# Edge scores of a graph attention layer: a one-hot of 112 rows plus 16 rows of block digits, a mask and one maximum, in place of a product and a sum

## What is computed

```python
xp = (layernorm(x) @ W).reshape(N, H, C)          # N = 3125, H = 4, C = 256
a_src = einsum('nhc,hc->nh', xp, att_src)         # one term a node and head
a_dst = einsum('nhc,hc->nh', xp, att_dst)
e = leaky_relu(a_src[src] + a_dst[dst], 0.2)      # a score for each edge and head
m = segment_max(e, dst)
alpha = exp(e - m[dst]) / segment_sum(exp(e - m[dst]), dst)[dst]
out = relu(segment_sum(xp[src] * alpha, dst) + bias)
x = x + out; x = x + moe_ffn(layernorm(x))
```

## Time and profile before

| | us |
|---|---|
| median of 3 runs | 2160.78 (2157.02 to 2161.48) |
| span of the profiled execution, the only time of it that is listed | 2296.1 |
| first stage, to the barrier | 0 to 332 |
| score stage | 332.1 to 482.6 |
| maxima, exponents, rest of the Gram matrix | 483 to about 590 |
| gather, norm, experts | to 2296.1 |

### The profile page before, as it was taken

The page is one execution under the profiler, slowest core; times in us unless marked ns, Lnnn a source line. Parts: engine busy times, 40 slices in busy tenths (PEclk is TensorE's granted clock), DMA queues, the critical chain, the costliest instruction groups (busy, mean ns, idle before and its releaser), DMA issues. The chain is left out here.

```text
span 2296.1 us, 53233 instructions
## 1 busy us (share of the span) xinstructions
PE 1959.2 (85%) x14846; PEld 1318.7 (57%) x14847; DVE 1470.6 (64%) x4341; ACT 1137.3 (50%) x2499; POOL 768.2 (33%) x943
## 2 busy tenths in 40 slices
PE   6999977667878888888888589983899999999997
PEld 4666545645766667777667455652454445555553
DVE  7988859987666666666666699867543443443333
ACT  4444421113666666676666566654543443443332
POOL 1020000022555555555555232321233333333332
PEclk9999976568999999999999889995899999999999
DMA  7444544403988888888888677746646556644542
GB/s 272 134 143 136 172 131 172 186 0 114 312 281 291 286 299 287 294 296 287 287 298 294 235 249 240 228 142 234 233 169 249 212 167 239 221 160 171 176 162 80
DMA packets 135664, 490.15 MB, mean 213 GB/s; under 512 B 16900, under 2 KB 17108, under 8 KB 133410
## 3 DMA queue, kind: packets, MB, share of 16 engines
q0 software_dynamic: 95568, 334.62, 43.5%
q1 hardware_dynamic: 31954, 125.15, 15.1%
q10 hardware_dynamic: 8064, 29.36, 3.7%
HBM read 419.17 MB, written 81.17 MB: 218 GB/s over the span
## 5 line engine op out<-in xcount | busy, mean ns | idle before, releaser
L1130 PE MATMUL main_ps<-rows,O 128*128 128x256 f16 x4992 | 619.2, 283 | 125.7 <-DVE acc L1066 66.3
L1113 ACT ACTIVATE O<-O,pk 128x128 f16<-128x128 f16 x1664 | 502.9, 387 | 246.1 <-DVE O L1083 203.5
L1130 PEld LDWEIGHTS main_ps<-rows,O 128*128 128x128 f16 x4992 | 480.9, 102 | 217.9 <-issue 72.8
L1052 POOL DMA_INDIRECT rows<-projected,idx x416 | 395.5, 951 | 325.2 <-PE small_ps L1135 202.9
L1087 DVE TENSOR_SCALAR O<-O,pk 128x128 f16<-128x128 f16 x1664 | 314.6, 273 | 15.0 <-issue 0.2
L1837 PE MATMUL x_h<-w_p,gram 128*128 x1344 | 307.1, 386 | 18.4 <-ACT gram L1787 7.6
L1852 PE MATMUL x_o<-w_p,gram 128*128 x1344 | 308.0, 379 | 1.4 <-ACT gram L1806 1.4
L1886 PE MATMUL pj_ps<-gram,xsT 128*125 128x512 f16 x1200 | 271.1, 385 | 8.8 <-ACT xsT L402 5.5
L1837 PEld LDWEIGHTS x_h<-w_p,gram 128*128 128x128 f16 x1344 | 131.6, 99 | 171.6 <-issue 31.5
L1886 PEld LDWEIGHTS pj_ps<-gram,xsT 128*125 128x125 f16 x1200 | 163.2, 139 | 104.7 <-ACT xsT L402 8.6
L1083 DVE TENSOR_SCALAR O<-iota,pk 128x128 f16<-128x128 f16 x416 | 109.4, 263 | 164.9 <-PE small_ps L1135 124.1
(11 more groups left out here) (346 smaller groups left out, 2538.9 us busy)
## 6 DMA issues: line engine op xcount, KB each, us to landing
w_f<-in_L_ffn_W_dram SPq DMA_DIRECT2D x14, 2048.0 KB
b_t<-in_L_ffn_b_dram ACTq DMA_DIRECT2D x56, 512.0 KB
projected_f<-xp_f POOLq DMA_DIRECT2D x25, 500.0 KB, 3.7
projected<-xp POOLq DMA_DIRECT2D x25, 500.0 KB, 4.6
out_dram<-n_x SPq DMA_DIRECT2D x25, 500.0 KB
x_after_gnn_normed<-PK POOLq DMA_DIRECT2D x25, 500.0 KB, 9.1
xt<-in_x_dram SPq DMA_DIRECT2D x24, 512.0 KB, 3.3
n_own<-projected_f SPq DMA_DIRECT2D x24, 512.0 KB, 13.0
```

The lines of the kernel that those rows point to most:

```text
L1052: pool.indirect_dma_start(out=rows[:, 4 * p + k, :, :].rearrange("k n d -> k (n d)"), out_offset=None, in_=xp_d[:, :], in_offset=bass.Indi ...
L1113: ins = act.activation(O[:, k, 1 + HEADS + h, :], O[:, k, 0, :], ACT.Copy, scale=pk[:, p, k, w:w + 1])
L1130: pe.matmul(main_ps[:, h * C:(h + 1) * C], O[:, k, 1 + HEADS * a + h, :], rows[:, 4 * p + k, b, h * C:(h + 1) * C], start=first and h % 2 ...
```

## The change

Source nodes are numbered by blocks of 112 rows in place of 125 (28 blocks in place of 25). The one-hot gets all 128 partitions: rows 0 to 111 tell the row in the block, and 16 more rows tell the block by two digits of base 7 (`digits_d`: 8 rows for the block number divided by 7, 8 for the rest). The matrix that it is multiplied with (`terms`) holds the node terms in its first 112 rows and, in the 16 digit rows, -65504 wherever the digit is not the block's (`digit_mask`). So every candidate but the right one comes out hugely negative, and DVE takes one maximum out of 112 columns a visit.

- DVE: the product `pick`, its sum and the eight `high_one_hots` go; one `tensor_reduce` with max reads PSUM directly. New are `digit_mask` (18 small instructions at i = 16), five more instructions in `edge_numbers`, one copy at the stage's end (`terms`); one of three `turned_numbers` goes.
- PE: 112 columns and 128 rows in place of 100 and 125 for each of the 832 source products, a third PSUM buffer for them (it waits for the maximum three groups ago), chunks 2 to 7 written out, 53 small products at the end of the first stage that move `st16` from blocks of 125 to blocks of 112 rows, four transposes fewer.
- SP: each chunk is loaded by three transfers (112, 16 and 128 partitions) in place of two, and two more tables are stored to DRAM.

```diff
-HI = -(-NODES // P)
+LOW, TENS, DIGITS = 112, 7, 8
+HI = -(-NODES // LOW)
+MASK = -65504.0
...
+        def load_numbers(sp, lo, dl, vs, done):
+            sp.dma_start(lo[0:LOW], lo_d[vs, :].partition_broadcast(LOW)).then_inc(done, 16)
+            sp.dma_start(lo[LOW:P], digits_d[:, vs, :].rearrange("n v k -> n (v k)").unsqueeze(1).broadcast_to([2, DIGITS, CHUNK * P])).then_inc(done, 16)
+            sp.dma_start(dl, dloc_d[vs, :].partition_broadcast(P)).then_inc(done, 16)
...
-                        if i in (15, 17, 19):
+                        if i in (15, 17):
                             turned_numbers((i - 15) // 2)
+                        if i == 16:
+                            digit_mask()
-                        if 17 <= i < 25:
-                            high_one_hots(i - 17)
...
+                    dve.wait_ge(s_spread, 1)
+                    dve.tensor_copy(terms[:, :, :, :], spread_ps)
...
+                    pe.matmul(spread_ps, ident16[:, :], mask[:, :, :, :], start=True, stop=True, skip_group_check=True)
+                    for n, blocks in enumerate((range(LATE), range(LATE, BLOCKS))):
+                        pe.wait_ge(s_st16, 2 * n + 2)
+                        for b in blocks:
+                            for a in range(ROWS * b // LOW, (ROWS * (b + 1) - 1) // LOW + 1):
+                                w = P - (ROWS * b - LOW * a)
+                                ins = pe.matmul(spread_ps[0:LOW, :, a, :], shift16[0:ROWS, w:w + LOW], ...
...
-                        for t, d in ((lo_b, lo_d), (dl_b, dloc_d)):
-                            sp.dma_start(t[p], d[CHUNK * i:CHUNK * (i + 1), :].partition_broadcast(P)).then_inc(s_row[p], 16)
+                        load_numbers(sp, lo_b[p], dl_b[p], slice(CHUNK * i, CHUNK * (i + 1)), s_row[p])
...
-                        dve.wait_ge(s_row[p], 32 * (j + 1))
-                        dve.tensor_scalar(lo_b[p], lo_b[p], iota_col[:, 0:1], None, ALU.is_equal)
+                        dve.wait_ge(s_row[p], 48 * (j + 1))
+                        dve.tensor_scalar(lo_b[p], lo_b[p], src_row[:, 0:1], None, ALU.is_equal)
...
-                            dve.tensor_tensor(pick[:, b, :, :, :], s_ps[b]..., hi_oh[:, four(n), :]..., ALU.mult).then_inc(s_sel, 1)
-                        dve.tensor_reduce(sT[:, four(n), :], pick[:, b, :, :, :], AX.X, ALU.add).then_inc(s_got, 1)
+                            dve.tensor_reduce(sT[:, four, :], s_ps[b][:, :, :].rearrange("k v (a h) -> k v h a", h=HEADS), AX.X, ALU.max).then_inc(s_got, 1)
...
-                            if not early(n, 2):
-                                pe.wait_ge(s_sel, n - 1)
+                            if n >= 3:
+                                pe.wait_ge(s_got, n - 2)
...
-                    steps(pe, 8, body)
+                    for i in range(8):
+                        body(i, i // 2, i % 2)
```

More of the change, by code:

```diff
@@ L226, in program @@
         early_ctx = ExitStack()
-        hiT = sbuf(early_ctx, "hiT", [P, VISITS], F16)
-        hi_oh = PK[:, :, :].rearrange("k v n -> k (v n)").bitcast(U8)[:, 0:VISITS * HI].rearrange("k (v a) -> k v a", a=HI)
+        src_row = sbuf(early_ctx, "src_row", [P, 1])
+        terms = sbuf(early_ctx, "src_terms", [P, 2, HI, HEADS], F16)
         dstV = sbuf(early_ctx, "dstV", [VP, ROW4])
@@ L591, in term_parts, with digit_mask @@
                         dve.tensor_tensor(st16[:, bs, 2 * HEADS:], stN[:, bs, :], st16[:, bs, 0:2 * HEADS], ALU.subtract).then_inc(s_st16, 1)
[L593 to L599, removed]
+                    def digit_mask():
+                        dve.memset(shift16[:, 0:P], 0.0)
+                        dve.memset(shift16[:, 2 * P:], 0.0)
+                        dve.tensor_copy(shift16[:, P:2 * P], ident)
+                        link(dve.tensor_scalar(digit[:, 0:1], iota_col[:, :], LOW - 0.5, -float(LOW), ALU.is_gt, ALU.mult))
+                        link(dve.tensor_scalar(digit[:, 1:2], iota_col[:, :], LOW + DIGITS - 0.5, -float(DIGITS), ALU.is_gt, ALU.mult))
+                        link(dve.tensor_tensor(digit[:, 2:3], digit[:, 0:1], digit[:, 1:2], ALU.add))
+                        link(dve.tensor_tensor(src_row[:, :], iota_col[:, :], digit[:, 2:3], ALU.add))
+                        link(dve.tensor_scalar(digits_of[:, 0, :], iota_row[:, 0:HI], 1.0 / TENS, -0.5 * (TENS - 1) / TENS, ALU.mult, ALU.add))
+                        link(dve.tensor_scalar(digits_of[:, 0, :], digits_of[:, 0, :], WHOLE, None, ALU.add))
+                        link(dve.tensor_scalar(digits_of[:, 0, :], digits_of[:, 0, :], -WHOLE, None, ALU.add))
+                        link(dve.scalar_tensor_tensor(digits_of[:, 1, :], digits_of[:, 0, :], -float(TENS), iota_row[:, 0:HI], ALU.mult, ALU.add))
+                        dve.tensor_scalar(digit[:, 3:4], iota_col[:, :], LOW - 0.5, MASK, ALU.is_gt, ALU.mult)
+                        link(dve.tensor_scalar(digit[:, 1:2], iota_col[:, :], LOW + DIGITS - 0.5, None, ALU.is_gt))
+                        link(dve.tensor_tensor(digits_of[:, 1, :], digits_of[:, 1, :], digits_of[:, 0, :], ALU.subtract))
+                        link(dve.scalar_tensor_tensor(digits_of[:, 2, :], digits_of[:, 1, :], digit[:, 1:2], digits_of[:, 0, :], ALU.mult, ALU.add))
+                        link(dve.tensor_scalar(digits_of[:, 0, :], digits_of[:, 2, :], src_row[:, :], digit[:, 3:4], ALU.not_equal, ALU.mult))
+                        for part in range(2):
+                            dve.tensor_copy(mask[:, part, :, :], digits_of[:, 0, :].unsqueeze(2).broadcast_to([P, HI, HEADS]))
@@ L859, in body @@
                                 skip_runtime_bounds_check_because="the table counts the borders at or below a visit, of which there are BLOCKS - 1")
-                            if not early(n, 2):
-                                pe.wait_ge(s_sel, n - 1)
+                            if n >= 3:
+                                pe.wait_ge(s_got, n - 2)
                             for u in range(4):
                                 for part in range(2):
-                                    h0 = 2 * HEADS * part
-                                    pe.matmul(s_ps[(p + q) % 2][:, u, :].rearrange("k (a h) -> k a h", h=HEADS), lo_b[p][0:ROWS, 4 * q + u, :],
-                                              st16[:, :, h0:h0 + HEADS], start=(part == 0), stop=(part == 1))
+                                    pe.matmul(s_ps[n % 3][:, u, :], lo_b[p][:, 4 * q + u, :],
+                                              terms[:, part, :, :].rearrange("r a h -> r (a h)"), start=(part == 0), stop=(part == 1))
                             if not early(n, 2):
```

65 lines of the change are left out of this document (36 added, 29 removed).

## The result

The changed kernel takes 2197.9 us (median of 4 runs, 2192.9 to 2200.6) against 2158.9 us (2156.9 to 2161.5): ratio 1.0173, 95% interval 1.0156 to 1.0191. The forecast was 2171 us, with 2147 to 2180 as its range. The sign was right; the added time is four times the 10.2 us of the sum. The comparisons here therefore use e1.

What follows compares the result with a forecast made beforehand. DVE seemed to bind the score stage, with the load's landing cycle right behind. Score stage +6.7 us and first stage +3.5 gave +10.2 us on 2160.8, so 2171 us, range 2147 to 2180.

Steps and rivals of the forecast that it cites:

- The sign: Whole kernel: slower than before the change, given a chance of 0.62.
- The view of the cycle: Score stage: a faster DVE uncovers load issue, landing, one-hots, last groups, next load; period = landing + 5.6 us.
- The engine count: Digits' load in each chunk: carried by two DMA engines, not sixteen, showing 34 small packets a chunk; chance 0.69.
- The landing: Chunk loads: two engines carry seven rows more, +3.5 to +3.9 us, so landing 14.6 us (13.8 to 15.7).
- the rival: Digits' load spread over all sixteen engines: landing 11.5 us, period 17.1, kernel 2149 us (2143 to 2153); chance 0.22.
- Chunks 1 to 6: Score stage: period 20.2 us for 18.06 in six chunks, +12.8 us (+8 to +19.4).
- Chunk 0: Score stage's first chunk: load landed long before its one-hots, one group less stands behind, -1.4 us.
- Chunk 7: Score stage's last chunk, no load to wait for: PE's groups 0.94 us apart, 12.8 us for 17.5, -4.7.
- The maximum: DVE's one reduce a group in the score stage, 448 values from PSUM: 0.62 to 0.64 us.
- the rival of a slow read: DVE's maximum, read from PSUM with stride four, takes 1.1 us: +4 us on the forecast; no chance of its own.
- The first stage: Stage before the scores: build_first waits for a later two-engine landing, +3.5 us (+3 to +5); on sixteen engines 0.
- the forecast's case at its dearest: Upper end of the two-engine case for the whole kernel: +18 us, 2179 us; chance of two engines 0.69.

Runs made afterwards that it cites:

- e1: The kernel before the change, unchanged, a single profiled run beside the others: 2161.1 us.
- e10: Changed kernel without the digits' load, low numbers broadcast to all 128 partitions, so its scores are wrong: 2145.9 us.
- e9: Changed kernel, both number tables broadcast to 128 partitions, 16 digit rows loaded over partitions 112 to 127 once the low numbers landed; local one-hots first: 2155.3 us.
- e3: Changed kernel with the digits loaded by two loads of 8 partitions, one for each table, in place of one: 2178.5 us.
- e12: Changed kernel with the same three loads of a chunk, the two-engine digits' load moved last, behind the local numbers: 2171.1 us.
- e4: Changed kernel with each digit stored eight times, as a table of 16 rows, so the digits' load is on sixteen engines: 2164.6 us.
- e2: Kernel before the change, with only the broadcast of the low numbers split into loads of 112 and 16 partitions: 2178.5 us.
- e7: Kernel before the change, with the broadcast of the low numbers split into two loads of 64 partitions: 2185.5 us.
- e5: Changed kernel with low numbers and digits in one table of 16 rows, loaded to 128 partitions by one load, each row repeated 8 times: 2181.0 us.
- e11: As e9, but the digits of chunks 1 to 7 issued from POOL's queue and the low numbers' one-hots first: 2164.3 us.

## Why the prediction was right in sign and wrong in size

- **The view of the cycle.** Right. DVE's work was covering a cycle of issue, landing, one-hots, last groups; once DVE is faster, the landing sets the period. Period = landing + 5.6: measured 18.96 + 5.46 in after, 11.66 + 5.46 in e10, 13.33 + 5.45 in e9.
- **The engine count.** Right: 34 small packets. The Trainium skill ("DMA: Bandwidth & Descriptors", section "Why a DMA increments its semaphore by 16 and not by 1") has the rule that was weighed there; the trace agrees. e3, e12 and e4 price the count.
- **The landing: the step that failed.** "One row takes 0.55 us of an engine", and then "seven rows more are +3.5 to +3.9 us". The price of a row was taken from 128-partition broadcasts and laid on every row of loads of 112 and 16. The bytes stayed the same, the places did not. Landing 18.96 us, for 14.6 (13.8 to 15.7). In periods: to split off the 16, on sixteen engines, costs 19.63 - 17.27 = 2.36 us (e4 - e10), for 0 to 0.36 forecast in the rival; two engines in place of sixteen, digits last, 20.90 - 19.63 = 1.27; the digits ahead of the local numbers 24.11 - 20.90 = 3.21 more. The sum knew of one of the three, and gave it 3.5.
- **Chunks 1 to 6.** Forecast +12.8; measured 6 x (24.11 - 18.00) = +36.7. The 23.9 us between them are most of the 28.8 by which the forecast missed (39.0 less 10.2). The last of the six chunks is taken at the mean of the other five.
- **Chunk 0.** Forecast -1.4; measured 23.99 for 25.03 us, -1.0.
- **Chunk 7.** Forecast 12.8 us for 17.5. Measured: last sum at 517.18, less the chunk's beginning at 480.24 + 24.11, 12.8; e1, in the same way, 17.5. DVE's last sums come 0.95 us apart, for 0.94:

```profile
513.70 0.62 DVE L836 TENSOR_REDUCE sT<-s_ps 128x16 f32<-128x448 f32 x1 [0.32 <-PE d_ps L903]
514.60 0.62 DVE L836 TENSOR_REDUCE sT<-v_ps 128x16 f32<-128x448 f32 x1 [0.28 <-PE d_ps L903]
...
516.55 0.63 DVE L836 TENSOR_REDUCE sT<-s_ps 128x16 f32<-128x448 f32 x1 [0.28 <-PE d_ps L903]
```

- **The maximum.** Forecast 0.62 to 0.64 us, measured 0.62 (DVE group of L836, 384 to 504 us: count, busy us, mean ns, idle), so the rival of a slow read didn't happen:

```profile
L836 DVE TENSOR_REDUCE sT<-s_ps 128x16 f32<-128x448 f32 x44 | 27.1, 623 | 9.2 <-PE d_ps L903 8.8
```

- **The first stage.** Forecast +3.5 (+3 to +5). The load of chunk 1 is issued at 335.72, for 332.07 in the profiled execution before and 329.31 in e1: +3.7 to +6.4. Of the two stalls forecast near i = 14 and 17 one came, of 1.8 us; the second was 0.2. None of the 0.67 of the earlier trace rows is left, and one of 11.20 us stands behind build_first (forecast: 7 or more), whose load landed 21.5 us after its issue at 265.38, for 14.2. So the same step failed here too. In e10, which has the rest of the first stage's changes, the load of chunk 1 is issued at 328.36, as in e1 within the 2.8 us between the two profiled executions of before (329.31 and 332.07).

```profile
286.86 1.95 DVE L644 TENSOR_SCALAR stage<-stage,src_row 128x6656 f16<-128x6656 f16 x1 [11.15 <-DMA stage<-dst_local_by_visit]
...
181.85 1.05 PE L1938 MATMUL tr_ps<-ident,xs 125*128 125x125 f16 x16 [1.82 <-DVE xs L502]
216.69 1.05 PE L1938 MATMUL tr_ps<-ident,xs 125*128 125x125 f16 x16 [0.21 <-DVE xs L502]
295.75 1.86 PE L1938 MATMUL tr_ps<-ident,xs 125*128 125x125 f16 x16 [11.20 <-DVE xs L502]
```

- **The added sum.** -1.0 + 36.7 - 4.7 + 6.4 = +37.4 against e1, and the stages behind, to which nothing was done, differ by 2.3 (1681.7 for 1679.3, before rounding), within the 4.6 us over which the four runs of before lie: 39.7, the difference of the two spans (2198.9 - 2159.2) and, within a microsecond, of the medians.
- **The range.** Its upper end, 2180, was the forecast's case at its dearest (2179) and a microsecond. The unknown cost of a load of another shape was bounded by rows of one shape only. A bound of "twice the row" for a load that the trace doesn't have would have reached past 2198: by estimate, 16 + 7 rows at 1.0 us in place of 0.5 are some +11 us a chunk.

## What to carry to other kernels

Bytes and engines alone don't price a load: how many partitions it writes, and in what pattern, does too. A broadcast to 128 partitions cut into 112 and 16 has the same bytes and lands a fifth later (14.2 us after the first issue in e2, 11.7 in e1), and a narrow load queued ahead of a wide one slows the wide one too, so keep wide loads whole and put the narrow one last, or over a wide one that has landed. When a change gives a hidden transfer another shape, measure that shape alone before summing, because what was hidden can be the bound once the change works, as it was here.

## What the runs showed of the hardware that was not expected

- A row of 13,312 B, DMA engines all busy: 0.51 us in a 128-partition broadcast of one row, 0.71 to 0.75 in one of 112, 1.02 in one of 64, 1.58 in the stretch of one of 16, 2.05 in that of two of 8 (e1, e2, e12, e7, e3, after).
- A load of 16 source rows x 8 repeats to 128 partitions: 1.01 us a row (e5), though both sides divide by 16.
- Order of the same three loads, one of them on two engines: 27 us of a kernel, 3.2 us a chunk (after and e12).
- A transfer of 208 KB issued from POOL while SP's 128 rows are under way lands 5.5 to 7.7 us after its issue in e11's seven chunks; from SP behind them (e9) 5.9 to 8.1.
- One DMA engine of sixteen can end later than the others although the two loads are alike for all: share 0.07 from 395 to 397 us in e10.
